# Reordering the start and one pipeline step of a fused linear-attention and mixture-of-experts layer

## Chip, cores, metric

One core of a Trainium2 chip runs the whole program. The metric is the device time of one execution in microseconds (us); lower is better.

## What is computed

The reference, cut down (x is 2 x 2048 x 256 in fp32, 4 heads of 64, chunks of C = 64 tokens; 2 shared and 8 routed experts of width 1024, the best 2 routed ones per token):

```python
x = x + attn(layernorm(x))
x = x + ffn(layernorm(x))
# attn
q, k, v = (silu(causal_conv4(x @ W)) for W in (Wq, Wk, Wv))
q, k = q / norm(q), k / norm(k)                 # over the 64 of a head
Kb, Vb = K * sigmoid(x @ Wb), V * sigmoid(x @ Wb)
A = einsum(Kb, K)                               # C x C in each chunk, summed over heads
T = inverse of (I + tril(A, -1))                # by rows in the reference
W, U = T @ Kb, T @ Vb
for each chunk: u = U - W * diag(S); o = q * diag(S) + tril(sum(q * k)) * u; S += k.T @ u
out = (o * rsqrt(mean(o * o) + eps) * g) @ Wo
# ffn
out = x + sum_shared gelu(x @ Wfc) @ Wproj + sum_top2 weight * gelu(x @ Wfc_r) @ Wproj_r
```

## The kernel before

The tokens go in 8 groups of 512 through a software pipeline written out in Python (`run_attention`). It has 12 steps t = 0 to 11 of 16 slots each. In step t the stage `ahead` normalises group t and turns it (columns on partitions); `front` of group t-1 makes the projections, the convolutions, K's normalisation and the chunk matrix A; `back` of group t-2 inverts it by doubling (products Y, Z and turned copies XT); `tail` of group t-3 makes the output, its normalisation per head, the product with Wo and the second layernorm (`x2n`). `up` (t-4) and `down` (t-5) are the shared experts for half of each group. From step 5 to step 8 all stages are there; step 9 has no `front`, step 10 only the last `tail`, `up` and `down`. After the pipeline (from 614.8 us) the rest of the experts runs.

Each engine has its own instruction stream, in the same order of slots. Inside a slot TensorE takes down, up, back, tail, front, ahead; the other engines take back, tail, front, ahead, down, up, and then `extras` (splits of expert weights into two fp16 halves). Nothing is reordered at run time: an instruction that waits holds its engine.

PSUM banks are handed round in rings. `front` has two banks, filled in the order of `FRONT_FILLS`: projections 2, 3, 6, 7, 4, 5, then `ssq` (sums of squares of K by head), projection 0, `tokK0`, `tokK1` (K turned to tokens), projection 1, `KT0`, `KT1`, `AT` and so on. A fill waits until the fill two places before it has been read out (`fr.empty`).

The lines that the change touches:

- SyncE loads x of group 0, then ten constants on one semaphore `const_in` (L629); GpSimd, ScalarE, TensorE and VectorE all wait for all ten.
- At the start ScalarE makes the high fp16 half of the projection weights (L917), VectorE the low half (L1487); then VectorE takes the statistics of x (L1493, L1497, L1500), GpSimd the power -0.5 (L842), VectorE L1694, ScalarE normalises (L1059).
- `front`, slot 4: TensorE makes projection 5 and the head sums of K's squares (L1192, 16 matmuls of 2 columns; squares by ScalarE L934). ScalarE copies the sums (L974), GpSimd takes the power (L796), VectorE scales K with it (L1538, slots 5 and 6). Projection 0 is in slot 5.
- `tail`, slots 3 to 7: ScalarE squares the output (L1025), GpSimd adds Q's squares (L824), TensorE makes head sums (L1192, slot 5), VectorE copies them (L1656), GpSimd takes the power (L828, in slot 5 of the tail), ScalarE spreads it (L1029), TensorE turns it (L1176, slot 7).
- `tail`, slots 9 to 11: VectorE takes the statistics of the sum (L1493, L1497, L1500), GpSimd the power (L832), VectorE makes `nmr2` (L1675), ScalarE normalises (L1038). GpSimd's masks (L804) follow L832 in its stream.
- Slot 8: ScalarE normalises the next group (L1059) and then makes the Gelu of `up` (L1068, with a table load) and its high half (L1073); VectorE makes the low half (L1705). TensorE's up product L1345 of chunk c+2 waits for the low half of chunk c.
- `EARLY_AT`: weight splits (ScalarE L1108, VectorE L1861) in the odd slots of steps 9 and 10.

Of the kernel before, what the change touches and what calls it, by code (L numbers as in the profile page):

```python
# [39 lines left out]
CONSTS_IN = 16 * 10  # L40
# [20 lines left out]
def row_tile(n, h):  # L61
# [23 lines left out]
EARLY_AT = {(slot, t): (SLOTS_A // 2) * (t - GROUPS - 1) + slot // 2  # L85
            for t in (GROUPS + 1, GROUPS + 2) for slot in range(1, SLOTS_A, 2)}
# [11 lines left out]
class Ring:  # L98
# [33 lines left out]
    [(f"proj{m}", "act") for m in PROJ_ORDER[:6]]  # L132
    + [("ssq", "act"), (f"proj{PROJ_ORDER[6]}", "act")]
# [166 lines left out]
def build(nc, x, w_proj, conv_w, g_col, w_o, cent, bias, w_ffn,  # L300
          ident, lvl_masks, eye2, head_sel, head_ones, block_tri, row_iota, tile_iota, pref, lane_iota, col_iota, tok_base, part_iota, out):
    ctx = ExitStack()
    with ctx:
# [159 lines left out]
        const_in = sem("const_in")  # L463
        consts_made = sem("consts_made")
# [150 lines left out]
        def _(sp):  # L615
# [167 lines left out]
        def _(pool):  # L783
# [6 lines left out]
            pool.wait_ge(const_in, CONSTS_IN)  # L790

            def front(slot, n, b):
                if slot == 4:

                    pool.wait_ge(*fr.empty(n, "ssq"))
                    pool.tensor_tensor(ssq, ssq, minus_half[:, 0:GT * NH], ALU.pow).then_inc(rnorm, 1)  # L796
                if slot == 9:

                    pool.wait_ge(at_kept, n + 1)
                    if n:  # L800

                        pool.wait_ge(*bk.full(n - 1, f"Y{LEVELS - 1}"))
# [12 lines left out]
            def tail(slot, n, b):  # L815
# [96 lines left out]
        def _(act):  # L912
            act.wait_ge(consts_made, CONSTS_MADE)
            act.wait_ge(const_in, CONSTS_IN)

# [8 lines left out]
            def front(slot, n, b):  # L924
# [25 lines left out]
                if slot == 0:  # L950
                    if n >= 2:

                        act.wait_ge(hist_set, n - 1)
# [16 lines left out]
                if slot == 4:  # L970
                    silu(3)
                    project(5)
                    act.wait_ge(*fr.full(n, "ssq"))
                    act.copy(ssq, fr.bank("ssq")[:, 0:GT * NH]).then_inc(fr.empty(n, "ssq")[0], 1)  # L974
                if slot == 5:
# [3 lines left out]
                    project(0)  # L979
                    silu(4)  # L980
# [69 lines left out]

            def ahead(slot, n, b):
                if slot == 8:
                    act.wait_ge(nmr_ready, n + 1)
                    if n:

                        act.wait_ge(*fr.full(n - 1, "tokK1"))
                        act.wait_ge(*ah.full(n - 1, "xnT1"))
                    for k in range(GT):
                        act.activation(xn[:, k], xl[:, k], ACT.Identity, bias=nmr[:, k:k + 1],  # L1059
                                       scale=rstd[:, k:k + 1]).then_inc(xn_ready, 1)  # L1060
# [50 lines left out]
            def extras(slot, t):  # L1111
                split_piece(slot, t)
# [44 lines left out]
        def _(pe):  # L1157
            pe.wait_ge(consts_made, CONSTS_MADE)
            pe.wait_ge(const_in, CONSTS_IN)

# [35 lines left out]
            def front(slot, n, b):  # L1196
# [9 lines left out]
                if slot == 0:  # L1206
                    if not n:
                        pe.wait_ge(wp_low, DB + 1)
# [6 lines left out]
                if slot == 4:  # L1215
                    project(5)

                    pe.wait_ge(squares, DB * (n + 1))
                    head_sums(fill(fr, n, "ssq"), sqK).then_inc(fr.sem_full, 1)
                if slot == 5:  # L1220
                    project(0)
# [256 lines left out]
        def _(dve):  # L1478
            dve.wait_ge(consts_made, CONSTS_MADE)
            dve.wait_ge(const_in, CONSTS_IN)  # L1480

            for d in range(DB):
                dve.tensor_scalar(wo[:, d], wo[:, d], gcol[:, d:d + 1], None, ALU.mult).then_inc(wo_scaled, 1)
# [518 lines left out]
```

## Time and profile before

| what | value |
| --- | --- |
| median of 3 runs | 1305.85 us |
| lowest, highest | 1302.28, 1309.93 us |
| profiled execution, its own time | 1308.97 us |
| its span | 1307.2 us |
| busy: TensorE, VectorE, ScalarE, GpSimd | 1155.9, 698.1, 622.1, 364.5 us |

The busy times are sums over the span. TensorE is busy 88% of it, but a busy time of matmuls at half clock counts double for the same work, and in the pipeline its idle time hangs on the other engines. PE is TensorE, PEld its weight loads, DVE VectorE, ACT ScalarE, POOL GpSimd, SP SyncE.

### The profile page before, as it was taken

How to read it: one execution, taken by the hardware profiler on the slowest of the kernel's cores; microseconds unless marked ns; L12 is line 12 of the kernel's file. 1: busy time of each engine (PE TensorE's matmuls, PEld its weight loads, DVE VectorE, ACT ScalarE, POOL GpSimd, SP SyncE). 2: the span in 40 equal slices, each digit the busy share in tenths (PEclk: the TensorE clock that was granted, in tenths of full speed). 3: DMA queues.
4: the chain of work that ended last, by engine and by line, in shares of the span. 5: the costliest groups of instructions: out<-in, count | busy, mean ns of one | idle time of the engine just before them, and what ended most of it. 6: DMA issues, size and time to landing. Idle time of an engine off the chain costs nothing.

```text
span 1307.2 us, 25625 instructions
## 1 busy us (share of the span) xinstructions
PE 1155.9 (88%) x9320; PEld 979.8 (75%) x9321; DVE 698.1 (53%) x1195; ACT 622.1 (48%) x1117; POOL 364.5 (28%) x294
## 2 busy tenths in 40 slices
PE   2696889999989899878899899999999999995886
PEld 1465668778777778767788788999999999993665
DVE  2668766765666666666788523333333333333444
ACT  2665546656465646456444634444444444441221
POOL 0315333334252425222012111111111112116542
PEclk9787878999899989989999999999999999997888
DMA  3112020102020102254222411111111111134443
GB/s 123 49 33 65 7 67 17 58 9 73 9 73 10 57 3 95 73 177 141 64 73 84 135 34 34 50 50 49 48 48 48 48 48 48 48 93 134 138 129 102
DMA packets 59529, 86.37 MB, mean 66 GB/s; under 512 B 7233, under 2 KB 49089, under 8 KB 59329
## 3 DMA queue, kind: packets, MB, share of 16 engines
q1 hardware_dynamic: 52160, 65.42, 15.7%
q0 software_dynamic: 7296, 19.93, 5.6%
q8 instruction: 52, 0.85, 0.3%
q14 instruction: 21, 0.16, 0.0%
HBM read 60.16 MB, written 25.17 MB: 65 GB/s over the span
## 4 chain that ended last, share of the span: by engine, by line
PE 68%; DVE 17%; ACT 6%; issue 5%; POOL 2%; DMA 0%; SPq 0%; DVEq 0%; ACTq 0%; POOLq 0%
PE ps L1365 25%; PE ps L1345 23%; DVE W L1523 4%; PE ps L1202 4%; PE ps L1192 3%; PE ps L1356 3%; PE ps L1264 2%; PE ps L1271 2%; PE ps L1423 2%; DVE late_room L1705 1%; DVE W L1615 1%; PE ps L1325 1%; POOL W L804 1%; PE ps L1176 1%; PE ps L1307 1%
## 5 line engine op out<-in xcount | busy, mean ns | idle before, releaser
L1365 PE MATMUL ps<-W,late_room 128*128 (+1 forms) x3264 | 388.5, 278 | 19.6 <-issue 19.0
L1345 PE MATMUL ps<-late_room,W 128*128 128x256 f16 x3072 | 369.6, 280 | 36.2 <-DVE late_room L1705 20.9
L1365 PEld LDWEIGHTS ps<-W,late_room 128*128 128x128 f16 x3264 | 324.9, 100 | 71.3 <-issue 28.3
L1345 PEld LDWEIGHTS ps<-late_room,W 128*128 (+1 forms) x3072 | 305.9, 100 | 87.3 <-DVE late_room L1705 26.0
L1068 ACT ACTIVATE ps<-ps 128x512 f32<-128x512 f32 x272 | 158.7, 583 | 407.4 <-PE ps L1345 358.5
L1705 DVE SCALAR_TENSOR_TENSOR late_room<-ps,late_room 128x512 f16<-128x512 f32 x272 | 181.5, 688 | 249.2 <-ACT late_room L1073 230.7
L1073 ACT ACTIVATE late_room<-ps 128x512 f16<-128x512 f32 x272 | 155.8, 596 | 2.5
L1523 DVE SCALAR_TENSOR_TENSOR W<-W 128x512 f32<-128x512 f32 x144 | 122.1, 849 | 8.7 <-ACT W L941 5.3
L1202 PE MATMUL ps<-W 128*128 128x512 f16 x384 | 101.5, 409 | 1.5 <-DVE W L1699 1.5
L922 ACT COPY W<-ps 128x512 f32<-128x512 f32 x112 | 61.0, 589 | 46.8 <-PE ps L1264 34.6
L904 POOL DMA_INDIRECT W<-ys_d,pos_i x64 | 62.1, 970 | 56.4 <-DVE W L1902 18.3
L1927 DVE TENSOR_SCALAR late_room<-ps 128x512 f32<-128x512 f32 x36 | 24.9, 692 | 97.9 <-PE ps L1365 97.9
L1202 PEld LDWEIGHTS ps<-W 128*128 128x128 f16 x384 | 40.0, 107 | 42.0 <-issue 12.0
L939 ACT ACTIVATE W<-ps 128x512 f32<-128x512 f32 x48 | 28.4, 592 | 79.4 <-PE ps L1202 78.4
L1176 PE MATMUL ps<-idt,W 128*128 128x128 f32 x256 | 39.4, 297 | 28.5 <-ACT W L1059 20.7
L861 POOL COPY gath<-idx 128x2 int32 x26 | 4.7, 182 | 201.7 <-PE ps L1423 201.7
L1719 DVE SCALAR_TENSOR_TENSOR late_room<-ps,late_room 128x512 f32<-128x512 f32 x32 | 22.0, 688 | 71.3 <-PE ps L1365 53.1
L1192 PE MATMUL ps<-W 128*128 128x2 f32 x256 | 38.8, 282 | 24.0 <-ACT W L934 16.1
L1192 PEld LDWEIGHTS ps<-W 128*128 128x128 f32 x256 | 38.2, 236 | 28.7 <-ACT W L934 20.4
L1264 PE MATMUL ps<-W 128*128 128x128 f32 x320 | 49.2, 302 | 10.6 <-DVE W L1573 8.9
L848 POOL DMA_INDIRECT late_room<-x2n_d,gath x52 | 50.0, 961 | 28.4 <-POOL gath L861 20.4
L1264 PEld LDWEIGHTS ps<-W 128*128 128x128 f32 x320 | 45.1, 215 | 15.7 <-DVE W L1573 11.7
(178 smaller groups left out, 1375.4 us busy)
## 6 DMA issues: line engine op xcount, KB each, us to landing
wstage<-in_w_ffn SPq DMA_DIRECT2D x40, 512.0 KB, 3.7
ys_d<-late_room SPq DMA_DIRECT2D x36, 256.0 KB
late_room<-in_x SPq DMA_DIRECT2D x8, 512.0 KB, 4.8
W<-in_x SPq DMA_DIRECT2D x8, 512.0 KB, 4.2
x2n_d<-W SPq DMA_DIRECT2D x8, 512.0 KB, 3.2
base_d<-W SPq DMA_DIRECT2D x8, 512.0 KB, 4.1
late_room<-base_d SPq DMA_DIRECT2D x16, 256.0 KB
acc_d<-late_room SPq DMA_DIRECT2D x12, 256.0 KB
```

The source lines that it names most:

```text
L904: pool.indirect_dma_start(out=yrow[k % YROWS][:, c], out_offset=None, in_=ys_d, in_offset=bass.IndirectOffsetOnAxis(ap=pos_i[:, c, t:t + 1 ...
L922: act.copy(dst, ring.bank(name)).then_inc(ring.empty(n, name)[0], 1)
L1068: act.activation(up_bank(n, c), up_bank(n, c), ACT.Gelu, scale=1.0 / (X_SCALE * W_SCALE)).then_inc(gelu_done, 1)
L1073: act.activation(hs[b][:, 0, 2 * c:2 * c + 2].rearrange("p f t -> p (f t)"), up_bank(n, c), ACT.Copy, scale=H_SCALE).then_inc(h_high, 1)
L1176: by_tile(ring, n, name, lambda to, k: pe.transpose(to, src[:, k, d * P:(d + 1) * P], idt[:]))
L1192: last = pe.matmul(dst[:, at:at + P // HD], src[:, d, k * P:(k + 1) * P], headsel, start=True, stop=True)
L1202: last = pe.matmul(to, wp[:, hw, d, m * P:(m + 1) * P], xnT[:, hx, d], start=(q == 0), stop=(q == len(parts) - 1))
L1264: by_tile(bk, n, f"Y{s}", lambda to, k: pe.matmul(to, CT[:, s - 1, k], X[b][:, k], start=True, stop=True))
L1345: last = pe.matmul(up_bank(n, c)[:, f * XT:(f + 1) * XT], weight(slot, d, hw, cols), x_halves[:, hx, d], start=(q == 0), stop=(q == len(pa ...
L1365: last = pe.matmul(down_bank(b)[:, c * D:(c + 1) * D], hs[b][:, hh, f, c * P:(c + 1) * P], weight(slot, DB + f // 4, hw, cols), start=(q = ...
L1523: dve.scalar_tensor_tensor(conv_at(m, b), pre[:, m, t:t + GRP], cw[:, m, t:t + 1], conv_at(m, b), ALU.mult, ALU.add).then_inc(conv_step, 1)
L1705: dve.scalar_tensor_tensor(lo, up_bank(n, c), H_SCALE, hi, ALU.mult, ALU.subtract).then_inc(h_low, 1)
```

## The change

- The loads at the start: `ident`, then `w_proj`, each on a semaphore of its own, then the other eight on `const_in`. ScalarE waits at the start for `w_proj` only, TensorE for `ident`, VectorE for none (its weight halves and scalings move into `prepare()`, behind slot 6 of step 0); the wait for the other constants moves to their first use.
- Projection 0 moves from slot 5 to slot 4 on TensorE and ScalarE, and K's head sums from slot 4 to slot 5, there behind `down`, `back` and the output's head sums (TensorE's order inside a slot). In the ring `ssq` and projection 0 change places. GpSimd takes K's power in slot 5 and the output's power in slot 6.
- The sum of squares of the output (L824) moves from GpSimd, slot 3, to VectorE, slot 4.
- The normalisation of the next group (L1059) moves behind the Gelu and high half of slot 8.
- Of the second layernorm's statistics the joining part (L1497, L1500) moves to the end of slot 9, behind `front`'s L1556 and L1559 and the low half L1705.
- The eight splits of step 10 move from slots 1, 3, 5, 7, 9, 11, 13, 15 to 3, 4, 5, 7, 10, 11, 13, 15.

```diff
-EARLY_AT = {(slot, t): (SLOTS_A // 2) * (t - GROUPS - 1) + slot // 2
-            for t in (GROUPS + 1, GROUPS + 2) for slot in range(1, SLOTS_A, 2)}
+EARLY_AT = {(2 * q + 1, GROUPS + 1): q for q in range(SLOTS_A // 2)}
+EARLY_AT |= {(slot, GROUPS + 2): SLOTS_A // 2 + q for q, slot in enumerate((3, 4, 5, 7, 10, 11, 13, 15))}
...
-    [(f"proj{m}", "act") for m in PROJ_ORDER[:6]]
-    + [("ssq", "act"), (f"proj{PROJ_ORDER[6]}", "act")]
+    [(f"proj{m}", "act") for m in PROJ_ORDER[:7]]
+    + [("ssq", "act")]
...
-            for dst, src in ((wp_stage, w_proj), (cw, conv_w), (idt[:], ident), (masks, lvl_masks),
-                             (minus2i, eye2), (wo, w_o), (gcol, g_col), (cen, cent), (headsel, head_sel),
-                             (headones, head_ones)):
+            sp.dma_start(idt[:], ident).then_inc(ident_in, 16)
+            sp.dma_start(wp_stage, w_proj).then_inc(proj_in, 16)
+            for dst, src in ((cw, conv_w), (headsel, head_sel), (masks, lvl_masks), (minus2i, eye2),
+                             (headones, head_ones), (wo, w_o), (gcol, g_col), (cen, cent)):
                 sp.dma_start(dst, src).then_inc(const_in, 16)
...
-                if slot == 4:
+                if slot == 5:
                     pool.wait_ge(*fr.empty(n, "ssq"))
                     pool.tensor_tensor(ssq, ssq, minus_half[:, 0:GT * NH], ALU.pow).then_inc(rnorm, 1)
...
-                if slot == 3:
-                    pool.wait_ge(q_sq, DB * (n + 1))
-                    pool.wait_ge(o_own_sq, DB * (n + 1))
-                    pool.tensor_tensor(osqT, osqT, qsqT, ALU.add).then_inc(o_sq, 1)
-                if slot == 5:
+                if slot == 6:
                     pool.wait_ge(*tl.empty(n, "oss"))
...
             act.wait_ge(consts_made, CONSTS_MADE)
-            act.wait_ge(const_in, CONSTS_IN)
+            act.wait_ge(proj_in, 16)
...
                     project(5)
+                    project(0)
+                if slot == 5:
                     act.wait_ge(*fr.full(n, "ssq"))
...
             def extras(slot, t):
+                if slot == 8 and t < GROUPS:
+                    normalise(t)
...
                 if slot == 4:
                     project(5)
+                    project(0)
+                if slot == 5:
                     pe.wait_ge(squares, DB * (n + 1))
                     head_sums(fill(fr, n, "ssq"), sqK).then_inc(fr.sem_full, 1)
-                if slot == 5:
-                    project(0)
                     turn_out(fr, n, "tokK0", Kr, 0)
...
+                if slot == 4:
+                    dve.wait_ge(q_sq, DB * (n + 1))
+                    dve.wait_ge(o_own_sq, DB * (n + 1))
+                    dve.tensor_tensor(osqT, osqT, qsqT, ALU.add).then_inc(o_sq, 1)
...
                 if slot == 9:
                     dve.wait_ge(*tl.empty(n, "attn1"))
-                    layer_stats(n, xr, bn2, mv2, rstd2, stats2)
+                    tile_stats(xr, bn2, stats2)
...
+                if (slot, t) == (6, 0):
+                    prepare()
+                if slot == 9 and 0 <= t - 3 < GROUPS:
+                    joined_stats(t - 3, bn2, mv2, rstd2, stats2)
```

## Rows read from the trace of the kernel before

**Rows 1.** Windows, steps 5 to 8 and step 7: PE busy, then other engines

```profile
236.90:515.70 278.80, 255.84 (x1930) 214.09 (x1930) 180.50 (x338) 163.91 (x299) 101.12 (x51) 0.94 0.11 35
377.70:446.10 68.40, 62.37 (x487) 52.42 (x486) 46.50 (x88) 41.69 (x77) 24.49 (x14) 0.98 0.11 33
```

**Rows 2.** Chain that ended last, step 7: start, length, what

```profile
394.83 2.93 DVE W L1523
...
402.07 4.08 PE ps L1365 x24
...
407.05 1.68 PE ps L1192 x16
408.73 1.32 PE ps L1202 x6
...
410.49 2.62 PE ps L1365 x24
```

**Rows 3.** Timeline, step 7, slots 3 to 7: start, length, engine

```profile
394.85 2.35 POOL L824 TENSOR_TENSOR W<-W 128x1024 f32<-128x1024 f32 x1 [11.07 <-ACT W L1025]
...
399.92 2.15 PE L1192 MATMUL ps<-W 128*128 128x2 f32 x16 [2.59 <-ACT W L934]
...
402.36 2.97 POOL L796 TENSOR_TENSOR W<-W 128x16 f32<-128x16 f32 x1 [5.16 <-ACT W L974]
...
409.02 3.34 POOL L828 TENSOR_TENSOR W<-W 128x16 f32<-128x16 f32 x1 [2.72 <-DVE W L1656]
...
411.10 0.68 DVE L1538 TENSOR_TENSOR W<-ps,W 128x512 f32<-128x512 f32 x1
...
415.00 1.06 ACT L1029 COPY W<-W 128x1024 f32<-128x1024 f32 x1
...
416.90 1.91 PE L1176 MATMUL ps<-idt,W 128*128 128x128 f32 x16
```

**Rows 4.** DMA issues, first 12 us: count, KB, us to landing

```profile
W<-in_w_proj SPq DMA_DIRECT2D x1, 1024.0 KB, 5.8
```

**Rows 5.** Timeline of the start

```profile
1.23 0.49 SPq L632 DMA_DIRECT2D W<-in_w_proj  x1
...
10.32 1.28 ACT L917 ACT_TABLE_LOAD   x1 [10.32 <-DMA W<-in_head_ones]
...
11.61 2.00 ACT L917 ACTIVATE W<-W 128x1024 f16<-128x1024 f32 x2
...
18.45 2.07 ACT L1059 ACTIVATE W<-late_room,W 128x256 f32<-128x256 f32 x4 [4.83 <-DVE W L1694]
```

**Rows 6.** Line L1609: VectorE, 128x1024 fp32, ns min/median/max

```profile
L1609 DVE TENSOR_TENSOR W<-W x8: 1224/1225/1227, 115.3 to 571.2; 128x1024 f32<-128x1024 f32 x8
```

**Rows 7.** TensorE windows in steps 7, 3 and 4, with granted clock

```profile
401.60:405.00 3.40, 3.40 (x18) 0.51 0.00 0
...
135.20:141.80 6.60, 6.60 (x27) 0.51 0.00 0
193.20:203.60 10.40, 10.40 (x46) 0.51 0.00 0
```

**Rows 8.** Timeline of step 7, slots 9 to 11

```profile
428.23 0.69 DVE L1705 SCALAR_TENSOR_TENSOR late_room<-ps,late_room 128x512 f16<-128x512 f32 x1 [1.25 <-ACT late_room L1073]
...
434.01 0.45 DVE L1675 SCALAR_TENSOR_TENSOR W<-W 128x4 f32<-128x4 f32 x1
...
434.50 2.08 ACT L1038 ACTIVATE W<-W 128x256 f32<-128x256 f32 x4 [1.44 <-DVE W L1675]
```

**Rows 9.** Timeline of step 3, slots 9 and 10

```profile
157.55 1.01 POOL L832 TENSOR_TENSOR W<-W 128x4 f32<-128x4 f32 x1 [16.27 <-DVE W L1500]
...
158.71 1.06 DVE L1675 SCALAR_TENSOR_TENSOR W<-W 128x4 f32<-128x4 f32 x1
```

**Rows 10.** Timeline of step 10, slots 1 to 5

```profile
572.31 3.02 DVE L1861 SCALAR_TENSOR_TENSOR W<-wstage,W 128x1024 f16<-128x1024 f32 x1
...
584.47 3.57 PE L1192 MATMUL ps<-W 128*128 128x2 f32 x16 [7.95 <-POOL W L824]
```

More of the change, by code:

```diff
@@ L799, in front @@
                     pool.wait_ge(at_kept, n + 1)
+                    if not n:
+                        pool.wait_ge(const_in, CONSTS_IN)
                     if n:
@@ L950, in front @@
                 if slot == 0:
+                    if not n:
+                        act.wait_ge(wp_low, DB + 1)
                     if n >= 2:
@@ L972, in front @@
                     project(5)
-                    act.wait_ge(*fr.full(n, "ssq"))
-                    act.copy(ssq, fr.bank("ssq")[:, 0:GT * NH]).then_inc(fr.empty(n, "ssq")[0], 1)
-                if slot == 5:
                     if n >= 2:
@@ L979, in front @@
                     project(0)
+                if slot == 5:
+                    act.wait_ge(*fr.full(n, "ssq"))
+                    act.copy(ssq, fr.bank("ssq")[:, 0:GT * NH]).then_inc(fr.empty(n, "ssq")[0], 1)
                     silu(4)
@@ L1049, in tail, with normalise @@
                     act.activation(xs[n % 2][:, 0], x2nT[:, :, 0:XT], ACT.Copy, scale=X_SCALE).then_inc(fed_high, 1)
-            def ahead(slot, n, b):
[L1052 to L1060, printed above, removed]
+            def normalise(n):
+                act.wait_ge(nmr_ready, n + 1)
+                if n:
+                    act.wait_ge(*fr.full(n - 1, "tokK1"))
+                    act.wait_ge(*ah.full(n - 1, "xnT1"))
+                for k in range(GT):
+                    act.activation(xn[:, k], xl[:, k], ACT.Identity, bias=nmr[:, k:k + 1],
+                                   scale=rstd[:, k:k + 1]).then_inc(xn_ready, 1)
+            def ahead(slot, n, b):
                 if slot in (10, 11):
@@ L1216, in front @@
                     project(5)
+                    project(0)
+                if slot == 5:
+                    if not n:
+                        pe.wait_ge(const_in, CONSTS_IN)
+                        pe.wait_ge(consts_made, CONSTS_MADE)
                     pe.wait_ge(squares, DB * (n + 1))
                     head_sums(fill(fr, n, "ssq"), sqK).then_inc(fr.sem_full, 1)
-                if slot == 5:
-                    project(0)
                     turn_out(fr, n, "tokK0", Kr, 0)
@@ L1478, in _, with prepare, tile_stats @@
         def _(dve):
[L1479 to L1483, printed above, removed]
[L1484 to L1490 removed]
+            def prepare():
+                for a in range(DB):
+                    dve.wait_ge(wp_high, a + 1)
+                    dve.scalar_tensor_tensor(wp[:, 1, a], wp_stage[:, a], W_SCALE, wp[:, 0, a],
+                                             ALU.mult, ALU.subtract).then_inc(wp_low, 1)
+                dve.wait_ge(consts_made, CONSTS_MADE)
+                dve.wait_ge(const_in, CONSTS_IN)
+                dve.tensor_scalar(cw_down, cw[:, :, TAPS - 1], 1.0 / (X_SCALE * W_SCALE), None, ALU.mult).then_inc(wp_low, 1)
+                for d in range(DB):
+                    dve.tensor_scalar(wo[:, d], wo[:, d], gcol[:, d:d + 1], None, ALU.mult).then_inc(wo_scaled, 1)
+            def tile_stats(src, b6, counted):
                 for k in range(GT):
```

20 lines of the change are left out of this document (8 added, 12 removed).

## The prediction

> **What bounds the kernel now.** I read the page's chain first, then the chain in order of time, then the timeline of single steps. After the pipeline TensorE works nearly without a gap on instructions that the diff leaves alone, so I look for nothing there. The pipeline is another matter. Steps 5 to 8 take 278.8 us together and step 7 alone 68.4 [rows 1]; in that step the chain goes from TensorE to VectorE to ScalarE and back [rows 2, 3]. Three places are to be seen. First, TensorE sits idle 2.59 us in front of K's head sums until ScalarE has the squares, and the squares are late because a convolution instruction of VectorE took 2.93 us; GpSimd ran its addition of 2.35 us at just that time [rows 2, 3]. Second, behind the idle time the granted clock falls to 1.2 GHz (0.51) [rows 7], so that 24 matmuls of `down` take 4.08 us where the next 24 take 2.62 [rows 2]. Third, VectorE waits 1.25 us in slot 9 for the first high half of `up`, which lies behind the next group's normalisation (four instructions, 2.07 us as in the start) [rows 5, 8]. At the start, ScalarE does nothing until 10.32 us, when the last constant has landed [rows 5].
>
> **The start (step 0).** `w_proj` is issued at 1.23 and lands 5.8 us later, at 7.0 [rows 4, 5]; now one issue of 0.49 lies before it, so 7.5. Table load 1.28 and two copies 2.00 end at 10.8. The statistics of x, GpSimd's power and `nmr` need only x, which was issued earlier and is half as large; they are ready by then. The normalisation starts at 10.8 instead of 18.45: 7.65 us. VectorE's low weight halves now follow ScalarE's copies while the normalisation runs and cost nothing; without that cover they would cost their own time, under 3 us. I take 7.5, bounds 6 and 8. All later queues shift with it.
>
> **K's head sums, and what passes them (steps 1 to 8).** I walk step 7 at full clock. Projection 5 is done at 399.92 - 2.59 = 397.33 [rows 3]. Projection 0 may go at once (its bank was read out by then): 1.32, to 398.65. Then comes `down`, 2.62, to 401.27; Z3, 0.90 (407.05 less the end of `down` at 406.15), to 402.17; the output's head sums, 1.68, to 403.85; K's, the same size, to 405.53 [rows 2]. The squares are long there: VectorE no longer meets GpSimd's addition, so the 2.93 loses most of the 2.35 that it stood beside [rows 2, 3]; against that stands VectorE's own new addition, 1.22 [rows 6]. Even with nothing saved, the squares were there at 399.92. That addition ends before TensorE wants it.
> What is late next: K's sums come 405.53 instead of 402.07. Behind them is GpSimd, which takes K's power first, 2.97, and then the output's, 3.34 [rows 3]. With 0.2 for the copy and the hand-overs: 408.7 and 412.05. ScalarE spreads in 1.06, to 413.15, and TensorE turns it then instead of at 416.90: **3.7 us earlier**. K is scaled from 408.7 instead of 411.10 [rows 3], so VectorE's last two convolutions come about 3 to 4 us earlier too. While ScalarE waits for K's sums, its Silu and TensorE's tokK wait behind, with slack.
> TensorE reaches slot 7 at about 412.5, 0.65 before the spread. If the clock falls once for 3.4 us at 0.51 [rows 7], it loses 1.7 us of work, of which 1.05 shows.
>
> **Slots 8 to 11 (steps 4 to 8).** Gelu, high half and low half come 2.07 earlier than the normalisation let them; VectorE's wait of 1.25 goes [rows 8]. The normalisation, 2.5 us later, is needed only in slot 10. But the joining part now comes behind two additions and a low half, and GpSimd's power (1.01) starts only after it, with nothing left to cover it: +1.0. In GpSimd's stream the masks follow the power at once, and then L1675, which starts in the same moment, meets them: it took 1.06 in step 3 and 0.45 in step 7 [rows 8, 9]. I take 1.06, +0.6 on step 7; lower bound 0. Here the Trainium skill, page "SBUF — State Buffer", Terms, says that VectorE and GpSimd lock their shared port pair for a whole instruction and the loser "fully blocks"; by that rule 1.06 would be the usual price, by step 7's row 0.45, and five steps would differ by 3 us. The second half thus gives 1.25 - 1.6 = -0.35, and step 7 comes to 3.7 - 0.35 = 3.35 without a fall of the clock, 2.3 with one: 65.05 or 66.1 us; a second stretch costs 1.7 more, 67.8.
>
> **How often the clock falls.** Two batches of head sums now stand together, 3.4 us of matmuls of 2 columns. In step 3, where K's and the output's sums stood with only Z3 between, the clock was at 0.51 from 135.2 to 141.8, in step 4 from 193.2 to 203.6 [rows 7], though TensorE was hardly idle. So I count with one stretch a step, two in every third: 66.7 us a step. 278.8 - 4 x 66.7 = 12.0 us for steps 5 to 8; bounds 18.6 (none) and 7.6 (two each).
>
> **Steps 1 to 4.** Step 1 has no work to put between; K's sums wait for projection 5's bank instead of the squares, 0, bounds -0.8 and +0.8 (half a batch of sums either way). Step 2 has no tail, so GpSimd has one power only: I estimate 2.5 from the same walk. Step 3 has no `down` to fill: GpSimd's two powers in line eat the gain, and slots 9 and 10 lose the uncovered 1.01 [rows 9]: a loss of 0.6, bounds -2 and +1. Step 4 gains 1.7, bounds 0 and 3. Together 3.6.
>
> **Steps 9 and 10.** In step 10 the split of slot 1 took 3.02 us, but the reduction behind it also waited for GpSimd's product, so only 1 us comes free [rows 10]. The same split, now in slot 3, stands in front of VectorE's new addition: ScalarE's high half, VectorE's low half 1.22, the addition 1.22, against GpSimd's 2.35 before. TensorE's sums start as before, at 584.47 [rows 10]. The later split also delays its staging buffer's next load, and SyncE's store of `x2n` stands behind such loads; ScalarE and VectorE wait there for GpSimd's power anyway (3.34 in step 7), which hides it. In slot 9 the split covered the power; now the joining comes later and nothing is won. 0, bounds -1.5 and +1.5.
>
> **Sum.** 7.5 + 3.6 + 12.0 + 0 = 23.1 us from the profiled execution's 1308.97. That execution is 3.1 above the median of 1305.85; from the median it makes 1282.8. I say **1283**.
>
> **Rivals.**
> (A) Likeliest, as above: 1283. Chance 0.55, own range 1276 to 1290.
> (B) The clock hardly falls, because TensorE's stall is gone: steps 5 to 8 give 18.6 and steps 2 to 4 about 2 more: 1274. For it speaks that step 7's output sums alone left no fall behind; against it, steps 3 and 4. 0.15.
> (C) The clock falls for two stretches or more at the joined sums, and waits that I have not seen take the place of the stall: 7.6 from steps 5 to 8, 1 from steps 1 to 4: 1290; with half of that, 1294. The Trainium skill, "TensorE: Matmul & The Clock Gate", Part 1 (What's actually happening), has the slow clock as the default that only activity lifts; by it, joined sums of 2 columns are a poor exchange for a stall. Steps 3 and 4 agree with that. 0.24.
> (D) Slower. GpSimd's two powers in line decide: the turned spread comes 7.6 us after K's sums. It is later than before once K's sums end after 409.3, 3.8 later than I have it; sums at half clock throughout are 3.4 of that. With another 2.5 us each step 1 to 8 would lose 2, more than the start gains: 1305.85 + 16 - 7.5 = 1314. 0.02.
> (E) Only the start works and the steps give nothing, since the chain has a branch that I priced too low: 1298. 0.04. That the moved splits do nothing is already in the sum.
>
> About 0.5% (6.5 us) is what a measurement of this kernel can tell from no change. Cases A to C and nearly all of E lie below 1299.3, so faster 0.95, same 0.03, slower 0.02. The range 1273 to 1296 leaves out D, E and the outer ends.
>
> **What would show it.** The first normalisation at about 10.8; TensorE's idle time before K's head sums near zero; no convolution of 2.9 us; the two powers of GpSimd back to back; L1675's successor near 1.06; step 7 near 66 us; the clock low for 3.4 us behind the joined sums. The prediction is wrong if the turned spread starts less than 2 us earlier than before in steps 5 to 8, if the projections at the start wait for something else than the normalised x, or if the part after the pipeline changes by more than 3 us.

## The result and the profile after

| | before | after |
| --- | --- | --- |
| median of 4 runs each, side by side | 1307.84 us | 1285.49 us (1284.11 to 1292.59) |
| ratio, 95% interval | | 0.9849 [0.9821, 0.9877] |
| profiled execution, its own time | 1308.97 us | 1284.79 us |
| its span | 1307.2 us | 1282.9 us |

The change made the kernel 1.5% faster, 22 us; 1283 was forecast. In short: the start came out as forecast, most of the rest comes from a wait of TensorE that is gone and from less time at half clock, and one of the six parts, the late joining of the statistics, costs more than it brings. Span and busy times from the page of the changed kernel:

```profile
span 1282.9 us, 25627 instructions
...
PE 1138.2 (89%) x9320; PEld 966.2 (75%) x9321; DVE 693.6 (54%) x1203; ACT 620.7 (48%) x1117; POOL 346.2 (27%) x286
```

TensorE is busy 17.7 us less for the same 9320 instructions: less of its work ran at half clock.

Lines have other numbers than in the kernel before: L1197 (head sums) was L1192, L1354 and L1374 (`up`, `down`) L1345 and L1365, L1181 L1176, L1031 L1029, L1693 (`nmr2`) L1675, L1724 (low half of `up`) L1705; L1718 is the low half of the normalised input. In the experiments they differ again by a few lines.

To place the gain I cut both executions where TensorE starts Z, K's first product of `tail` (16 matmuls of 128 columns), which is the first instruction of each step from step 3 on. "Rest" is from the start of step 10 to the end of the span.

| | first projection | start of step 3 | start of step 5 | steps 5 to 8 | step 9 | start of step 10 | rest |
| --- | --- | --- | --- | --- | --- | --- | --- |
| before | 25.79 | 109.18 | 236.71 | 278.85 | 50.56 | 566.12 | 741.08 |
| after | 18.42 | 100.95 | 225.60 | 264.52 | 51.89 | 542.01 | 740.89 |

So 7.4 us came from the start, 3.7 from steps 1 to 4 (11.1 by the start of step 5), 14.3 from steps 5 to 8; 1.3 were lost in step 9, and the rest did not move (0.2). The windows of steps 5 to 8 of the changed kernel, columns as in [rows 1] (granted clock third from the end):

```profile
225.60:291.63 66.03, 62.42 (x487) 52.29 (x485) 45.91 (x89) 41.47 (x77) 21.91 (x13) 0.97 0.13 42
291.63:359.49 67.86, 64.24 (x486) 53.70 (x485) 45.04 (x88) 41.37 (x77) 23.40 (x12) 0.95 0.13 39
359.49:425.50 66.01, 62.40 (x487) 52.67 (x486) 45.95 (x89) 41.47 (x77) 21.69 (x13) 0.97 0.10 33
425.50:490.12 64.62, 60.07 (x478) 50.63 (x477) 41.91 (x76) 38.21 (x71) 22.12 (x11) 1.00 0.12 34
```

Against the 0.94 of [rows 1] the clock is higher. Between 225 and 490 it is at half in one stretch of 3.4 us in step 5, two on end in step 6, one in step 7 and none in step 8: lengths follow their number, 64.6 us with none, 66.0 with one, 67.9 with two.

The start, from the timeline (against [rows 5]):

```profile
7.89 1.28 ACT L916 ACT_TABLE_LOAD   x1 [7.89 <-DMA W<-in_w_proj]
9.19 2.00 ACT L916 ACTIVATE W<-W 128x1024 f16<-128x1024 f32 x2
10.28 2.36 DVE L1492 SCALAR_TENSOR_TENSOR W<-W 128x1024 f16<-128x1024 f32 x2 [2.14 <-ACT W L916]
11.10 2.06 ACT L1061 ACTIVATE W<-late_room,W 128x256 f32<-128x256 f32 x4
```

ScalarE now waits for `w_proj` alone, and VectorE's low halves run beside the normalisation. Step 7, slots 4 to 7 (against [rows 2, 3]):

```profile
380.40 2.78 PE L1374 MATMUL ps<-W,late_room 128*128 128x256 f16 x24
380.80 1.21 DVE L1670 TENSOR_TENSOR W<-W 128x1024 f32<-128x1024 f32 x1
...
383.02 1.06 PE L1280 MATMUL ps<-W 128*128 128x128 f32 x8
383.91 3.96 PE L1197 MATMUL ps<-W 128*128 128x2 f32 x32
...
388.16 2.90 POOL L798 TENSOR_TENSOR W<-W 128x16 f32<-128x16 f32 x1 [6.82 <-ACT W L981]
388.62 3.69 PE L1374 MATMUL ps<-W,late_room 128*128 128x256 f16 x24
391.02 2.90 POOL L828 TENSOR_TENSOR W<-W 128x16 f32<-128x16 f32 x1
...
394.20 1.06 ACT L1031 COPY W<-W 128x1024 f32<-128x1024 f32 x1
...
396.10 1.91 PE L1181 MATMUL ps<-idt,W 128*128 128x128 f32 x16
```

Down, Z, then both batches of head sums as one group of 32, with no idle time in brackets; the next `down` (3.69 instead of 2.78) runs partly at half clock: the window 386.4 to 390.4 has a granted clock of 0.58. The turned output starts 36.61 us into the step; before it was 39.35 (416.90 less 377.55). Slots 9 to 11 of the same step (against [rows 8]):

```profile
406.10 0.68 DVE L1724 SCALAR_TENSOR_TENSOR late_room<-ps,late_room 128x512 f16<-128x512 f32 x1
...
411.91 1.01 POOL L832 TENSOR_TENSOR W<-W 128x4 f32<-128x4 f32 x1 [17.99 <-DVE W L1513]
412.89 5.30 POOL L809 TENSOR_TENSOR W<-W 128x512 f32<-128x512 f32 x5
412.95 1.04 DVE L1693 SCALAR_TENSOR_TENSOR W<-W 128x4 f32<-128x4 f32 x1 [1.12 <-POOL W L832]
413.92 0.68 DVE L1718 SCALAR_TENSOR_TENSOR W<-ps,W 128x512 f16<-128x512 f32 x1
...
414.65 0.66 PE L1181 MATMUL ps<-idt,W 128*128 128x128 f32 x4 [1.33 <-DVE W L1718]
```

The low half waits for nothing now. But VectorE stands 1.12 us for GpSimd's power, L1693 then takes 1.04 beside the masks, and L1718 behind it is what TensorE waits for, 1.33 us. That wait is new. TensorE's waits between 180 and 480 us (total, times, longest; before, 12.1 us on the squares in 5 waits and 12.3 on the low half in 7):

```profile
PE ps L1354 <- DVE late_room L1724: 9.4, 10, 1.6
PE ps L1181 <- DVE W L1718: 8.0, 8, 1.3
PE ps L1207 <- DVE W L1551: 0.9, 1, 0.9
```

And in step 9 the chain in order of time runs through a DMA queue:

```profile
477.03 1.01 POOL W L832
478.04 5.26 POOL W L809 x5
483.30 2.32 POOL W L836
...
485.64 2.91 DMA base_d<-W
...
489.53 5.97 DMA wstage<-in_w_ffn
...
495.52 1.07 ACT W L1112
```

The later power makes the masks and the base addition later, so the base store is issued later; in SyncE's queue the next load of expert weights stands behind that store, and ScalarE's split in front of the reduction waits for the load. ScalarE's wait itself is not new (2.8 us in the kernel before, 3.4 here), and of TensorE's time the later load takes 0.5: its wait 13 us into the step is 2.04 instead of 1.56. The larger part of the loss lies in slots 9 to 11, where TensorE waits for the low half 2.11 and 1.79 instead of once 2.72:

```profile
529.29 1.91 POOL L832 TENSOR_TENSOR W<-W 128x4 f32<-128x4 f32 x1 [14.88 <-DVE W L1513]
531.23 0.16 DVE L1693 SCALAR_TENSOR_TENSOR W<-W 128x4 f32<-128x4 f32 x1 [0.90 <-POOL W L832]
532.05 1.48 PE L1354 MATMUL ps<-late_room,W 128*128 128x256 f16 x12 [1.79 <-DVE late_room L1724]
```

The power takes 1.91 beside a weight split of VectorE, VectorE stands for it, and the low half stands behind that. Against this the clock never falls in step 9, where it was at half for 3.4 us before.

### The profile page after: what moved, and what is told of

It reads as the page before. It is cut to its first block, busy times and chain, and to the rows that moved or that the text cites. A ratio compares the mean times of both kernels' runs of the same rounds, so it can differ in the third digit from the quotient of the medians.

```text
span 1282.9 us, 25627 instructions
## 1 busy us (share of the span) xinstructions
PE 1138.2 (89%) x9320; PEld 966.2 (75%) x9321; DVE 693.6 (54%) x1203; ACT 620.7 (48%) x1117; POOL 346.2 (27%) x286
## 4 chain that ended last, share of the span: by engine, by line
PE 66%; issue 13%; DVE 9%; POOL 6%; ACT 4%; DMA 1%; SPq 0%; POOLq 0%; ACTq 0%; DVEq 0%
PE ps L1374 25%; PE ps L1354 22%; PE ps L1207 5%; PE ps L1365 3%; PE ps L1197 2%; POOL W L798 2%; PE ps L1273 2%; POOL W L828 2%; PE ps L1432 2%; POOL W L809 2%; PE ps L1280 1%; ACT W L1040 1%; PE ps L1334 1%; PE ps L1290 1%; DVE W L1536 1%
## 5 line engine op out<-in xcount | busy, mean ns | idle before, releaser
L1374 PE MATMUL ps<-W,late_room 128*128 (+1 forms) x3264 | 387.9, 278 | 22.0 <-issue 21.6
L1354 PE MATMUL ps<-late_room,W 128*128 128x256 f16 x3072 | 361.2, 276 | 31.8 <-DVE late_room L1724 18.9
L1374 PEld LDWEIGHTS ps<-W,late_room 128*128 128x128 f16 x3264 | 323.2, 99 | 75.5 <-issue 32.6
L1354 PEld LDWEIGHTS ps<-late_room,W 128*128 (+1 forms) x3072 | 302.3, 99 | 79.1 <-DVE late_room L1724 24.6
L1724 DVE SCALAR_TENSOR_TENSOR late_room<-ps,late_room 128x512 f16<-128x512 f32 x272 | 181.2, 687 | 242.5 <-ACT late_room L1077 224.5
L1536 DVE SCALAR_TENSOR_TENSOR W<-W 128x512 f32<-128x512 f32 x144 | 109.0, 758 | 9.7 <-ACT W L940 6.3
L1207 PE MATMUL ps<-W 128*128 128x512 f16 x384 | 98.2, 402 | 9.4 <-DVE W L1551 6.1
L1207 PEld LDWEIGHTS ps<-W 128*128 128x128 f16 x384 | 38.9, 104 | 52.3 <-issue 10.8
L1181 PE MATMUL ps<-idt,W 128*128 128x128 f32 x256 | 39.7, 297 | 32.1 <-DVE W L1718 16.1
L1181 PEld LDWEIGHTS ps<-idt,W 128*128 128x128 f32 x256 | 30.8, 153 | 38.3 <-DVE W L1718 19.7
L848 POOL DMA_INDIRECT late_room<-x2n_d,gath x52 | 50.1, 963 | 28.4 <-POOL gath L861 20.4
L1273 PEld LDWEIGHTS ps<-W 128*128 128x128 f32 x320 | 43.9, 209 | 15.3 <-DVE W L1586 11.2
L809 POOL TENSOR_TENSOR W<-W 128x512 f32<-128x512 f32 x40 | 46.3, 1191 | 23.6 <-ACT W L1002 23.6
L848 POOL DMA_INDIRECT late_room<-x2n_d,idx x20 | 19.2, 959 | 121.7 <-PE ps L1432 108.7
```

What stands on the lines that cost most here:

```text
L809: pool.tensor_tensor(CT[:, s - 1], AT, masks[:, s].unsqueeze(1).to_broadcast([P, GT, P]), ALU.mult).then_inc(masked, 1)
L848: pool.indirect_dma_start(out=xg[t.par][:, c], out_offset=None, in_=x2n_d, in_offset=bass.IndirectOffsetOnAxis(ap=rows, axis=0)).then_inc( ...
L1181: by_tile(ring, n, name, lambda to, k: pe.transpose(to, src[:, k, d * P:(d + 1) * P], idt[:]))
L1207: last = pe.matmul(to, wp[:, hw, d, m * P:(m + 1) * P], xnT[:, hx, d], start=(q == 0), stop=(q == len(parts) - 1))
L1273: by_tile(bk, n, f"Y{s}", lambda to, k: pe.matmul(to, CT[:, s - 1, k], X[b][:, k], start=True, stop=True))
L1354: last = pe.matmul(up_bank(n, c)[:, f * XT:(f + 1) * XT], weight(slot, d, hw, cols), x_halves[:, hx, d], start=(q == 0), stop=(q == len(pa ...
```

## Experiments

The runs came in three sets, each with the kernel before beside it. In the set of e5 to e8 the kernel before took 1309.72 us, as above; in the two others 1265.59 and 1268.48, and there "rest" is about 40 us shorter for every kernel (697 to 701 instead of 739 to 742), while the pipeline hardly differs: steps 5 to 8, which e1 leaves alone, take 278.5 us in e1 and 278.9 in the kernel before, in the other set. So kernels are compared by their ratio to before, and by the table of steps, which stands behind the last of them. Each row there is one execution, and e8 and e11 show what that can tell apart.

**e1: the start alone.** All else of the diff taken back.

```diff
-  projection 0 in slot 4, head sums of K in slot 5, addition on VectorE,
-  normalisation behind the Gelu, joined statistics late, splits moved
+  all as in the kernel before; kept: order of the loads, their semaphores, prepare()
```

> The kernel before with the new start alone (loads by need, own waits, the preparation behind slot 6). By the prediction's walk the first normalisation starts at about 11 us instead of 18.45 and nothing later takes it back: 7.4 us off, 1300.4 us. Rival: the weight loads behind the start or a step's DMA take part of it back: 1303 to 1306 us.

1260.39 us, ratio 0.9952 [0.993, 0.9975]. First projection 18.23, start of step 10 at 557.38, 8.7 us earlier; steps 5 to 8 take 278.5 as before. The start stands alone, and nothing in the pipeline gives it back; the medians differ by 5.2.

**e2: start and the addition on VectorE.** As e1, with L824's addition moved.

```diff
-                if slot == 3:
-                    pool.tensor_tensor(osqT, osqT, qsqT, ALU.add).then_inc(o_sq, 1)
+                if slot == 4:
+                    dve.tensor_tensor(osqT, osqT, qsqT, ALU.add).then_inc(o_sq, 1)
```

> As the kernel with the new start alone, and the sum of squares on VectorE too. If VectorE's 2.9 us convolution was GpSimd's addition standing beside it, no convolution is longer than 0.8 us, the squares come about 2.2 us earlier in steps 3 to 8 and TensorE's stall before K's head sums shrinks from 2.6 to under 0.6 us: 8 to 12 us off the kernel with the start alone, about 1290 us. Rival: VectorE's own addition of 1.22 us a step and the clock, which falls behind the head sums whatever the stall, eat it: 2 us or less off, 1298 us.

1236.17 us, ratio 0.9769 [0.9728, 0.981]: with two of the six parts the ratio is lower than with all of them, and the steps are clearer than the ratio. Step 10 starts at 533.28, 24.1 us earlier than in e1; steps 5 to 8 take 262.5 instead of 278.5. TensorE's waits:

```profile
PE ps L1353 <- DVE late_room L1724: 14.9, 9, 2.9
PE ps L1197 <- ACT W L933: 3.5, 4, 0.9
```

The wait on K's squares fell from 12 us to 3.5, though the head sums stand at their old place. In steps 5 to 8 alone these waits fell from 10.7 in e1 to 3.5, and the time at half clock from 30.7 to 10.2: the stall and the slow clock behind it went together.

**e3: K's head sums back** (slot 4; projection 0 in slot 5; the ring, ScalarE's copies and GpSimd's powers go back with them, not shown), all else as changed.

```diff
-                    project(0)
-                if slot == 5:
                     head_sums(fill(fr, n, "ssq"), sqK).then_inc(fr.sem_full, 1)
+                if slot == 5:
+                    project(0)
```

> The changed kernel with K's head sums and projection 0 back in their old places (and the two powers in their old slots). If the move is what removes the stall and shortens the steps: 8 to 12 us more than the changed kernel, 1294 to 1297 us. Rival: the sum of squares on VectorE had removed the stall already and the move only joins the two batches of head sums: within 3 us of the changed kernel, 1283 to 1288 us.

1246.58 us, ratio 0.9849 [0.9807, 0.989]; start of step 10 at 546.79, against 541.8 to 542.0 with the move. Steps 5 to 8 are the same (264.8): 3.5 us of waits on the squares come back, and 6.8 us less at half clock, worth 3.4, stand against them; of the 4.8 us, 0.8 lie ahead of step 3, 1.6 in it, 0.5 in step 4 and 1.7 in step 9.

**e4: K's head sums behind projection 0, still in slot 4.**

```diff
                     project(0)
+                    head_sums(fill(fr, n, "ssq"), sqK).then_inc(fr.sem_full, 1)
                 if slot == 5:
-                    head_sums(fill(fr, n, "ssq"), sqK).then_inc(fr.sem_full, 1)
```

> The changed kernel with K's head sums at the end of slot 4, right behind projection 0, so that down, Z3 and the output's sums come after them. If the two batches of head sums side by side are what brings the clock down behind them, it stays up in more steps, and K's power is taken 3.4 us earlier, so that GpSimd's second power is no longer behind it: 4 to 8 us less than the changed kernel, 1277 to 1281 us. Rival: the sums' place does not matter to the clock, or the wait for projection 5's bank (0.6 us) costs what is won: 1284 to 1288 us.

1237.87 us, ratio 0.9781 [0.974, 0.9822], start of step 10 at 536.87: better by 5 than slot 5, all of it ahead of step 5 (220.53 instead of 225.60). Steps 5 to 8 are again 264.2.

**e5: the changed kernel again**, in the set of e6 to e8.

> The changed kernel itself, on the chip that ran the others, whose part behind the pipeline is some 40 us shorter for every kernel. 1242 to 1248 us there, with the steps of the first profile: steps 5 to 8 together 262 to 267 us.

1286.58 us, ratio 0.9832 [0.9798, 0.9866]; steps as in the first execution within 0.2 us.

**e6: the joined statistics back in front.**

```diff
-                if slot == 9 and 0 <= t - 3 < GROUPS:
-                    joined_stats(t - 3, bn2, mv2, rstd2, stats2)
...
                     tile_stats(xr, bn2, stats2)
+                    joined_stats(n, bn2, mv2, rstd2, stats2)
```

> The changed kernel with the joining of the second layernorm's statistics back behind its tile statistics in slot 9. The kernel with only the new start and the sum on VectorE reached step 10 8.7 us earlier than the changed kernel, so some part costs. If it is this one (the power without cover, L1675's successor standing beside the masks, and in step 9 the loads behind the base store): 6 to 11 us less than the changed kernel, about 1236 us, and step 9 back from 51.9 to 50.6 us. Rival: the normalisation behind the Gelu is what costs; then 2 us or less come off here.

1274.32 us, ratio 0.9728 [0.9699, 0.9758], 12.3 below e5. Step 10 starts 9.5 us earlier (532.28), steps 5 to 8 take 259.9, step 9 is back at 50.56. Its slots 9 to 11 of step 7, beside those above:

```profile
402.65 1.01 POOL L832 TENSOR_TENSOR W<-W 128x4 f32<-128x4 f32 x1 [16.30 <-DVE W L1513]
403.63 5.43 POOL L809 TENSOR_TENSOR W<-W 128x512 f32<-128x512 f32 x5
403.81 0.68 DVE L1725 SCALAR_TENSOR_TENSOR late_room<-ps,late_room 128x512 f16<-128x512 f32 x1
404.41 0.45 DVE L1694 SCALAR_TENSOR_TENSOR W<-W 128x4 f32<-128x4 f32 x1
```

The power runs while VectorE does other work, the small instruction starts 0.8 us into the masks and takes 0.45, and no wait of L1181 is left. The late joining is the part of the change that costs. The wait it makes, L1181 for L1718, is 6.0 us over steps 5 to 8 of the changed kernel, 1.5 a step; that 4.6 come back and not 6.0 goes at least in part with the clock, which is at half for 20.5 us in e6 and 13.7 in the changed kernel.

**e7: the normalisation back in front of the Gelu.**

```diff
-                if slot == 8 and t < GROUPS:
-                    normalise(t)
...
             def ahead(slot, n, b):
+                if slot == 8:
+                    normalise(n)
```

> The changed kernel with the next group's normalisation back before the Gelu. If the joined statistics are what costs, this changes steps 4 to 8 by 1 us or less each in either way: 1243 to 1249 us. Rival: the later normalisation holds up TensorE's turning of it in slots 10 and 11 and costs 1.5 us a step: 1236 to 1239 us.

1289.17 us, ratio 0.9845 [0.9818, 0.9872], 2.6 above e5, within what the medians tell apart; in the steps it is clear, step 10 at 548.17 instead of 541.82, 6.3 later. Of these, 1.85 are in steps 5 to 8, the others in steps 3, 4 and 9.

**e8: e4 and e6 together.**

> K's head sums in slot 4 behind projection 0 and the statistics joined at once, all else as in the changed kernel. If both find their gains in different places, they add up: 5 us for the sums and 6 to 11 us for the statistics, 1229 to 1234 us, steps 5 to 8 together under 258 us. Rival: both take away the same slack (what sets a step is then TensorE alone): 1234 to 1237 us, no better than the better one of the two.

1272.95 us, ratio 0.9723 [0.9696, 0.975]; step 10 at 530.03, steps 5 to 8 260.9. The 5 us that the place of K's sums was worth in e4 are 2.3 here, and 1.3 by e11, which runs the same program up to step 10. That both bought the same slack is likely, and not shown.

**e9: the addition back on GpSimd**, slot 3, all else as changed (the reverse of e2's diff).

> The changed kernel with the sum of squares of the output back on GpSimd, slot 3. Theory 1 (the sum on VectorE is the largest earner, since GpSimd's 2.35 us addition holds VectorE's convolution instruction for 2.9 us and with it the squares): steps 5 to 8 together 275 to 282 us instead of 264.5, a convolution instruction of about 2.9 us back in each step, total 12 to 18 us above the changed kernel (ratio to before 0.992 to 0.998). Rival (the changed kernel's K sums behind one more projection have enough slack to hide the late squares, as my prediction had it: the stall itself is covered either way): steps 5 to 8 stay within 3 us of 264.5 and the total within 4 us.

1244.90 us, ratio 0.9833 [0.9798, 0.9868]. My theory 1 fell: steps 5 to 8 take 264.53, as in the changed kernel, and step 10 starts 2.9 us later. Step 7:

```profile
374.34 4.50 DVE L1541 SCALAR_TENSOR_TENSOR W<-W 128x512 f32<-128x512 f32 x3
375.14 2.37 POOL L829 TENSOR_TENSOR W<-W 128x1024 f32<-128x1024 f32 x1 [11.06 <-ACT W L1032]
...
382.26 3.63 PE L1202 MATMUL ps<-W 128*128 128x2 f32 x32
```

The stretched convolution is back (three take 4.50 instead of 2.32), and the squares are as late as before (done 22.3 us into the step in both), but the joined head sums start 2.1 us behind them, with the output's half first, and do not notice. With e2 this makes the picture for steps 5 to 8: one stall, two remedies. The move removes it whole, the addition all but 0.9 us a step, and with one in place the other wins nothing more there.

**e10: e6, and GpSimd takes the output's power ahead of K's.**

```diff
-                if slot == 6:
+                if slot == 5:
                     pool.wait_ge(*tl.empty(n, "oss"))
```

> Joined statistics back in front (as in the run that undid them: steps 5 to 8 259.9 us, step 10 starts at 532.28), and GpSimd takes the output's power ahead of K's. Theory 1 (GpSimd's two powers in line set the turned spread, as my prediction walked it): ScalarE's spread starts about 3 us earlier and steps 5 to 8 are 3 to 8 us shorter, about 254. Rival (in this order TensorE's own stream reaches the turned spread no earlier, as the trace of the changed kernel shows it without idle time before slot 7, and K's scaling comes later instead): steps 5 to 8 within 2 us of 259.9 or longer by up to 6 us, because VectorE's scaling of K and so tokK, projection 1 wait.

1235.71 us, ratio 0.9757 [0.9722, 0.9791]; steps 5 to 8 261.4 instead of 259.9, step 10 at 536.49 instead of 532.28. Step 7:

```profile
382.95 3.34 POOL L828 TENSOR_TENSOR W<-W 128x16 f32<-128x16 f32 x1 [4.72 <-DVE W L1674]
386.26 2.90 POOL L798 TENSOR_TENSOR W<-W 128x16 f32<-128x16 f32 x1
...
390.15 1.07 ACT L921 COPY W<-ps 128x512 f32<-128x512 f32 x2 [4.97 <-PE ps L1273]
391.11 1.06 ACT L1031 COPY W<-W 128x1024 f32<-128x1024 f32 x1
...
393.01 1.91 PE L1181 MATMUL ps<-idt,W 128*128 128x128 f32 x16
```

The output's power is ready at 386.3, and ScalarE spreads it at 391.1 all the same: ahead of it in ScalarE's order stands a copy that waits 4.97 us for TensorE's product Y. The turned output starts 36.62 us into the step, with either order of the powers. In all four steps of e10 the clock falls behind the head sums, so it does not try the order in a step where the clock stays up. Step 10 starts 4.2 us later than in e6, and step 3 alone is 4.2 longer (63.6 instead of 59.5).

**e11: e8 with the splits of step 10 back in the odd slots.**

```diff
-EARLY_AT |= {(slot, GROUPS + 2): SLOTS_A // 2 + q for q, slot in enumerate((3, 4, 5, 7, 10, 11, 13, 15))}
+EARLY_AT |= {(slot, GROUPS + 2): SLOTS_A // 2 + q for q, slot in enumerate((1, 3, 5, 7, 9, 11, 13, 15))}
```

> K's head sums in slot 4 behind projection 0, joined statistics undone (as in the last run of the batch before: 1272.95 us, step 10 starts at 530.03, last ZK to end 740.67), and the splits of step 10 back in the odd slots. Theory (the moved splits do nothing, as predicted: 0, bounds -1.5 and +1.5): steps up to 9 unchanged, from the start of step 10 to the end 740.67 within 1.5 us. Rival (split of slot 1 holds the reduction, so undoing costs what the change had won): 2 to 3 us longer from the start of step 10, total about 1275.5.

1232.48 us, ratio 0.974 [0.9703, 0.9777]. For the output's head sums of step 10, behind the step's start: 18.35 before and 18.34 in e1 (addition on GpSimd, old splits), 17.39 in e9 (GpSimd, moved splits), 19.20 in e2 and 19.19 in e11 (VectorE, old splits), 18.24 in the changed kernel (VectorE, moved). The moved splits win 0.95, the addition loses 0.85: the sum is 0.1. The rest of 701.31 against 697.92 in e12 is 3.4 us in one pair of executions, 1.1 of which stand by the end of the pipeline; where the other 2.3 are I did not find. All three executions with the old splits in the two sets with the short rest (e1, e2, e11: 699.6 to 701.3) lie above all five with the moved ones (697.3 to 698.0), so the moved splits may win some 2 to 3 us there; the kernel before and the changed one, with the long rest, differ by 0.2.

Step 9 is 2.15 longer than in e8: the load is as late as in the changed kernel (TensorE's wait is 2.04 again), and the clock is at half for two stretches of 3.4 us instead of one. This is no effect of the edit: up to step 10 both are one program, with the statistics joined early. In e11 the base store is issued 4.48 us ahead of the start of step 9, as in every kernel that joins late (4.48 or 4.49), and in all the others 5.36 to 5.76 ahead. So the late joining makes that load late in each of the five kernels that have it (six executions), but it can be late without it.

**e12: all parts but two.** K's head sums at the old place (as e3) and the joined statistics in front (as e6).

> Start, sum of squares on VectorE, normalisation behind the Gelu and the moved splits, with K's head sums at their old place and the joined statistics undone. Start and sum alone gave a start of step 10 at 533.28 us; the normalisation was worth about 6 us in the steps of the changed kernel. Theory 1 (the parts add up): step 10 starts at 528 to 531, total 1269 to 1273, so the move of K's sums was not needed once VectorE has the addition. Rival (K's sums need the move, worth 5 us as in the run that undid it): step 10 starts at 535 to 538, total 1276 to 1279.

1233.18 us, ratio 0.9744 [0.9712, 0.9775]; step 10 at 530.78, steps 5 to 8 259.7. Theory 1 held: without the late statistics the move of K's sums is worth nothing that one execution can tell (532.28 with it in e6).

The table of steps. "Turned" is the start of the turned output in step 7, behind the step's start; "half clock" is the time in steps 5 to 8 at the lower of the two clock levels. e5 is as the changed kernel within 0.2 us.

| kernel | K's sums | addition | normalise | joined | steps 5 to 8 | step 9 | step 10 starts | turned | half clock |
| --- | --- | --- | --- | --- | --- | --- | --- | --- | --- |
| before | slot 4 | GpSimd | first | first | 278.9 | 50.56 | 566.12 | 39.35 | 30.7 |
| e1 | slot 4 | GpSimd | first | first | 278.5 | 50.56 | 557.38 | 39.35 | 30.7 |
| e2 | slot 4 | VectorE | first | first | 262.5 | 50.56 | 533.28 | 35.96 | 10.2 |
| e12 | slot 4 | VectorE | behind | first | 259.7 | 50.56 | 530.78 | 35.97 | 13.7 |
| e6 | slot 5 | VectorE | behind | first | 259.9 | 50.56 | 532.28 | 36.63 | 20.5 |
| e10 | slot 5, power second | VectorE | behind | first | 261.4 | 50.56 | 536.49 | 36.62 | 23.9 |
| e8 | slot 4, behind proj. 0 | VectorE | behind | first | 260.9 | 50.56 | 530.03 | 35.82 | 17.1 |
| e11 | slot 4, behind proj. 0 | VectorE | behind | first | 259.7 | 52.71 | 530.99 | 37.48 | 13.7 |
| e4 | slot 4, behind proj. 0 | VectorE | behind | late | 264.2 | 52.10 | 536.87 | 37.48 | 6.8 |
| e3 | slot 4 | VectorE | behind | late | 264.8 | 53.55 | 546.79 | 35.96 | 6.8 |
| e9 | slot 5 | GpSimd | behind | late | 264.5 | 53.69 | 544.92 | 36.63 | 13.7 |
| e7 | slot 5 | VectorE | first | late | 266.4 | 53.75 | 548.17 | 35.47 | 13.7 |
| after | slot 5 | VectorE | behind | late | 264.5 | 51.89 | 542.01 | 36.61 | 13.7 |

e8 and e11 are one program up to step 10. Their step 7 starts at 350.56 and 346.92, its turned output 35.82 and 37.48 behind that, and steps 5 to 8 take 260.9 and 259.7. So e6, e8, e10, e11 and e12 are not told apart in steps 5 to 8; that e2 differs from e1 by 16 us and the early joining from the late one by some 4 to 5 stands well clear of this.

## Why the prediction came out, and where it did not

**The start: right.** 7.5 forecast, 7.4 measured at the first projection. The normalisation starts at 11.1 instead of 10.8, because `w_proj` landed 6.1 us after its issue at 1.77, where I had taken 5.8 from [rows 4]. The low halves cost nothing, as said.

**Steps 1 to 4: right in sum, not in parts.** 3.6 forecast, 3.7 measured. Steps 1 and 2 gave 0.9 where I had 2.5; step 3 gave 0.8 where I had a loss of 0.6; step 4 gave 2.05 (1.7 forecast).

**Steps 5 to 8: 12.0 forecast, 14.3 measured, by the number of clock stretches.** I gave 65.05, 66.1 and 67.8 us for none, one and two stretches in step 7, and the four steps measured 64.6, 66.0, 66.0 and 67.9. I counted one and a third per step, 5.3 in all; there were 4. By my own prices the steps as they came (one, two, one and none) make 265.05, 13.8 less than before: of the 2.3 that I was short, 1.8 are the count, and 0.5 are steps somewhat shorter than I had them. So this term of the sum was mis-sized mainly by its count, in the direction of case B.

**The two powers of GpSimd in line: right, and they decide only where the clock stays up.** Counted from the step's start, I had the second power end at 34.5 us, the spread at 35.6, and TensorE there 0.65 earlier; with one clock fall TensorE would come at 36.65, behind the spread. Step 8, the one step of the four without a fall, follows the first:

```profile
457.14 2.90 POOL L828 TENSOR_TENSOR W<-W 128x16 f32<-128x16 f32 x1
460.07 1.04 ACT L1031 COPY W<-W 128x1024 f32<-128x1024 f32 x1 [1.20 <-POOL W L828]
461.17 1.97 PE L1181 MATMUL ps<-idt,W 128*128 128x128 f32 x16 [0.35 <-ACT W L1031]
```

The power ends at 34.5, ScalarE waits for it, TensorE waits 0.35 for ScalarE, and the turned output starts at 35.67. Steps 5 and 7, with one fall, follow the second: TensorE has no idle time and starts it at 36.63 and 36.61, while the spread begins at 34.7. There the power is not what decides: in e10 the output's is ready 4.8 us before the spread, and nothing moves, since ScalarE's copy behind Y stands in front of the spread and TensorE's own stream arrives last. 2.65 us forecast for step 7, 2.74 measured.

**What bought it: only half seen.** I put the gain down to K's sums going behind other work, and noted that the squares would be there in time even with nothing saved. e9 shows this: with the addition on GpSimd steps 5 to 8 are the same 264.5. What I did not draw from it is the reverse: by freeing the convolution, the addition on VectorE removes 16 us from these steps alone (e1 to e2), and behind it the move of K's sums has nothing left to win (e6 and e12, 259.9 and 259.7). Of the time that came back, much is clock: 17.1 us less at half clock, which is 8.5 us of TensorE's work; the waits on the squares that are gone were 10.9 us of steps 5 to 8, and the new waits take part of both. The place was in [rows 2, 3], where the 2.35 us addition and the 2.93 us convolution stand together; I had given it no price, and so could not see that two parts of the change compete for it.

The Trainium skill, page "SBUF — State Buffer", Terms, has VectorE and GpSimd lock a shared port pair for a whole instruction. The trace agrees for the convolution: the three take 2.2 us longer when the GpSimd addition of 2.37 stands beside them (e9), and 2.32 without it.

**Slots 8 to 11: -0.35 forecast, and the loss is larger than that by itself.** The terms were +1.25 for the normalisation and -1.6 for the late joining, per step. e7 gives the first as 0.46 (1.85 over four steps), e6 the second as 1.15 (4.6 over four steps; its own wait is 1.5 a step). The mechanism was as forecast: power uncovered, L1693 at 1.04 (1.06 forecast) beside the masks. By its start against the masks, 0.06 behind them or 0.8, the same instruction takes 1.04 or 0.45.

**Step 9: missed, the term of the sum that failed outright.** 0 forecast, -1.3 measured. My ground was that in slot 9 the split covered the power and that the later joining wins nothing; it loses, since VectorE now waits 0.90 for the power with the low half behind it, 1.2 us of TensorE's time. And I had followed GpSimd's delay to the masks and not two steps on, to the store behind them in SyncE's queue and the load behind that store, 0.5 us. With the clock's part the step is 1.3 longer. e6 gives it back: 50.56. All six executions that join late have a longer step 9 (51.9 to 53.8); e11 (52.71) shows that the late load, and a step longer by the clock, can come without it.

**Step 10: right.** By my account "only 1 us comes free", and the addition takes it again: 0.95 and 0.85 by the pairs of e11, with 0.2 between the kernel before and the changed one from the start of step 10 to the end. Whether the moved splits win 2 to 3 us further on is open (e11).

**The rivals.** D did not come: K's sums ended 28.4 us into step 7, and D begins at 31.75 (409.3 in my walk). The total lies in A's own range; in steps 5 to 8 it went from A towards B, 14.3 between 12.0 and 18.6. The Trainium skill, "TensorE: Matmul & The Clock Gate", Part 1, has a clock that only activity lifts. The trace agrees so far. In steps 5 to 8 of the five kernels with joined sums (after, e6, e7, e9, e10), 17 steps of 20 have a fall that begins between 2.5 us before the end of the sums and 1.2 behind it, with no idle time ahead of them. In the six kernels with the sums apart and no long stall (e2, e3, e4, e8, e11, e12) K's sums have such a fall in 9 steps of 24, and the output's in none. Where they stand apart in e3 and e4, half clock is least of all (6.8 us). Yet neither is faster in these steps than the changed kernel: what e3 wins in clock it has in waits.

The best kernels are e6, e8, e11 and e12, ratios 0.9723 to 0.9744, some 1% under the changed kernel; their intervals overlap and they are not told apart. e12 needs the fewest edits of them. The start and the addition alone (e2, 0.9769 [0.9728, 0.981]) come within 3.3 us of the earliest start of step 10, and that interval overlaps theirs too.

## What to carry to other kernels

When one stall has two causes in line (a late producer, and a consumer placed early), two remedies buy it once; ask for each part what is left for it once the others stand. Before moving a wait, follow everything behind it in its engine's order in every kind of step, down to the stores and the loads behind them in a DMA queue. And which of two candidates sets an instruction can change with TensorE's clock: walk a step at both levels before an experiment is read as a no.

## What was unexpected

- A small VectorE instruction of 128x4 elements takes 0.15 to 0.16 us alone (L1713, eight times), 0.45 or 1.04 beside GpSimd's masks of about 1.06 us each, by when it starts.
- Steps differ by whole stretches of clock: 64.6, 66.0 and 67.9 us for the same instructions in the changed kernel, and an edit elsewhere, or none (e8 and e11), moves which steps have them; over steps 5 to 8 they sum to 6.8 us (e3, e4) up to 30.7 (before). The length does not always follow them: in e7 a step with one takes 67.4 us and one with two 65.7.
- The part behind the pipeline took 741 us in one set of runs and 698 in the others, of one and the same program text there. The last 103 us show a lower clock and less DMA traffic (129 GB/s) in the first case, and a clock of 0.97 with 174 GB/s in the second. The changed kernel:

```profile
1180.00:1282.90 102.90, 77.60 (x579) 58.84 (x577) 45.54 (x86) 26.00 (x48) 45.69 (x50) 0.83 0.44 129
```

and e9:

```profile
1140.00:1242.90 102.90, 89.22 (x797) 78.31 (x795) 58.88 (x111) 35.42 (x66) 68.61 (x74) 0.97 0.59 174
```

What makes the difference I could not try.
